# A graph kernel whose count steps start at every 4th node in place of every 8th

## What is computed

```
h  = relu(layernorm(x))
x  = x + relu([h, sum of h[src] by dst, sum of edge_attr by dst] @ W.T + b)
h  = relu(layernorm(x))
h1 = relu(mean of h[src] by dst  @ W1_l + b1 + h  @ W1_r)
x  = x + relu(mean of h1[src] by dst @ W2_l + b2 + h1 @ W2_r)
```

## Time and profile before

| | before |
|---|---|
| median of three runs | 1425.23 us |
| the profiled execution | 1426.45 us |
| its span in the trace | 1424.6 us |
| first step of the build loop starts | 113.0 us |
| last step of the build loop starts | 647.4 us |

### The profile page before, as it was taken

The page is one execution under the profiler, slowest core; times in us unless marked ns, Lnnn a source line. Parts: engine busy times, 40 slices in busy tenths (PEclk is TensorE's granted clock), DMA queues, the critical chain, the costliest instruction groups (busy, mean ns, idle before and its releaser), DMA issues.

```text
span 1424.6 us, 34949 instructions
## 1 busy us (share of the span) xinstructions
PE 1352.9 (95%) x12145; PEld 1227.3 (86%) x12146; DVE 807.9 (57%) x1830; ACT 492.1 (35%) x1398; POOL 645.4 (45%) x762
## 2 busy tenths in 40 slices
PE   3768999999999999999999999999999999999996
PEld 3657999999999999898888888888888888888885
DVE  8678999988988888883445445522222223222122
ACT  2731123455788888882333232311111110000000
POOL 5400001111112122126777776367777654777775
PEclk9688999999999999999999999999999999999998
DMA  6109778888899998895654564656656555666663
GB/s 185 28 4 255 204 221 242 236 250 244 265 273 271 273 280 263 263 278 184 231 184 162 192 222 125 210 180 200 204 188 214 184 184 189 210 216 214 220 219 87
DMA packets 284437, 293.91 MB, mean 206 GB/s; under 512 B 19317, under 2 KB 249920, under 8 KB 284384
## 3 DMA queue, kind: packets, MB, share of 16 engines
q1 hardware_dynamic: 233861, 212.90, 47.6%
q0 software_dynamic: 25728, 68.65, 16.3%
q10 hardware_dynamic: 24795, 11.74, 2.9%
HBM read 245.11 MB, written 48.11 MB: 206 GB/s over the span
## 4 chain that ended last, share of the span: by engine, by line
PE 88%; DVE 4%; ACT 3%; DMA 2%; issue 2%; POOL 2%; ACTq 0%; POOLq 0%; SPq 0%; DVEq 0%
PE edge_banks L1148 42%; PE edge_banks L1084 21%; PE banks L1058 10%; PE edge_banks L1125 4%; PE edge_banks L1080 4%; PE banks L1166 3%; POOL shared L882 2%; PE banks L946 1%; ACT own L1296 1%; DMA shared<-in_edge_attr 1%; PE edge_banks L1155 1%; PE banks L1160 1%; DVE edge_t L1508 1%; ACT shared L1353 1%; DMA shared<-g_rows,list_src 0%
## 5 line engine op out<-in xcount | busy, mean ns | idle before, releaser
L882 POOL DMA_INDIRECT shared<-g_rows,list_src x546 | 532.3, 975 | 232.9 <-issue 166.4
L1148 PE MATMUL edge_banks<-g_even,shared 128*128 128x257 f16 (+1 forms) x3822 | 443.4, 272 | 1.2 <-DVE shared L1776 1.2
L1148 PEld LDWEIGHTS edge_banks<-g_even,shared 128*128 128x128 fp8e3 x3822 | 371.6, 97 | 58.8 <-DVEq L1686 1.3
L1084 PE MATMUL edge_banks<-shared 128*128 128x128 f32 x2744 | 345.3, 276 | 5.2 <-issue 4.3
L1084 PEld LDWEIGHTS edge_banks<-shared 128*128 128x128 f32 x2744 | 325.8, 193 | 8.5 <-issue 8.1
L860 POOL DMA_DIRECT2D counts<-shared x156 | 76.5, 491 | 479.6 <-ACT shared L1353 464.7
L1737 DVE SCALAR_TENSOR_TENSOR shared<-edge_banks,shared,own 128x128 f32<-128x128 f32 x98 | 34.4, 351 | 362.2 <-PE edge_banks L1148 339.5
L1148 PE MATMUL edge_banks<-shared 128*128 128x256 f16 x1911 | 225.8, 272 | 0.2 <-DVE own L1719 0.2
L1653 DVE TENSOR_TENSOR shared<-iota,shared 128x3528 f16<-128x3528 f16 x98 | 195.4, 1994 | 38.9 <-PE banks L1058 38.5
L1353 ACT ACTIVATE shared<-banks 128x392 uint16<-128x392 f32 x312 | 152.1, 487 | 176.0 <-PE banks L1058 165.5
L1148 PEld LDWEIGHTS edge_banks<-shared 128*128 128x128 fp8e3 x1911 | 185.3, 97 | 30.7 <-DVE own L1719 0.5
(11 more groups left out here) (282 smaller groups left out, 978.1 us busy)
## 6 DMA issues: line engine op xcount, KB each, us to landing
shared<-in_edge_attr SPq DMA_DIRECT2D x195, 512.0 KB, 4.7
shared<-counts SPq DMA_DIRECT2D x117, 784.0 KB
counts<-shared POOLq DMA_DIRECT2D x156, 196.0 KB, 4.1
shared<-g_rows,list_src POOLq DMA_INDIRECT x546, 2.6
shared<-hot_rows SPq DMA_DIRECT2D x20, 304.0 KB
g_rows<-g_even SPq DMA_DIRECT2D x1, 3136.0 KB, 15.8
g_rows<-shared ACTq DMA_DIRECT2D x49, 64.0 KB
g_rows<-g_even ACTq DMA_DIRECT2D x49, 64.0 KB
```

Source lines behind the costliest of these rows:

```text
L882: pool.indirect_dma_start(ring_g[use % RING][:, t, 0:2 * D], None, g_rows[r], bass.IndirectOffsetOnAxis(ap=list_src[:, at:at + 1], axis=0) ...
L1084: mm = pe.matmul(edge_wide[bank][:, :, at], ring[:, bank * GROUP_TILES + j, :], hot_dst[u][:, k, (j - 1) * SPREAD:j * SPREAD].unsqueeze(1) ...
L1148: mm = pe.matmul(acc[s][:, 0:wide], stream8[slot][:, order[h], :], G[r % 2][:, order[h], 0:wide], start=h == 0, stop=h == BLOCKS - 1, skip ...
```

## The change

The window becomes 4 nodes wide. Counts go to the same memory in the same layout, and the other constants follow:

| | before | after |
|---|---|---|
| nodes of a window (`WIN`) | 8 | 4 |
| cells of a step, so columns of its matmul | 196 | 98 |
| stretches in a bank (`DUO`) | 2 | 4 |
| steps an iteration (`STEPS_IT`) | 18 | 20 |
| steps in the program | 1764 | 1960 |
| waits for a cleared bank in a half | 2 (before steps 1 and 6) | 1 (before step 1, for all ten) |
| window starts held by a partition (`PER`) | 7 | 10 |
| columns compared for each tile row (`MARKS`) | 912 | 1388 |
| indirect DMAs for the starts | 8 | 12 |
| blocks of 128 in the step tables (`SBLK`) | 14 | 16 |

The starts of the ten listed blocks get a column of their own (`STARTS` = `PER` + 2) in place of being picked out of all starts by seven matmuls. The edge sums, the bank count, the 312 copies and clears, and the rounds stay.

```
-WIN = 8
-DUO = 2
+WIN = 4
+DUO = 4
-SLOT = 256
-STEPS_IT = 18
+SLOT = 128
+STEPS_IT = 20
-PARTS = ((0, 5), (5, 9))
+PARTS = ((0, 5), (5, 10))
-PER = 7
+PER = 10
-SRC_BITS = 13
+SRC_BITS = 14
...
-            for j in range(PER + 1):
+            for j in range(STARTS):
                 pool.indirect_dma_start(rows8[:, j, :], None, keys_table, bass.IndirectOffsetOnAxis(ap=tw_i[:, j:j + 1], axis=0)).then_inc(S["rows8_in"], 16)
...
-                        for j in range(PER):
-                            pe.matmul(to[:, 72 + c:73 + c], pick_j[:, j, lists], first_e[:, j:j + 1], start=j == 0, stop=False, skip_group_check=True)
+                        pe.matmul(to[:, 72 + c:73 + c], pick[:, lists], first_e[0:LISTED, PER + 1:STARTS], start=True, stop=False, skip_group_check=True)
...
                         def steps(half, regs):
-                            for (lo, hi), until in zip(PARTS, regs[HALF:HALF + 2]):
+                            for lo, hi in PARTS:
                                 at = slots(regs[lo:hi])
-                                pe.wait_ge(S["zeroed"], until)
+                                if lo == 0:
+                                    pe.wait_ge(S["zeroed"], regs[HALF])
                                 for s in range(lo, hi):
...
                     def clear(j):
                         act.wait_ge(S["evacuated"], b * DPB + (j + 1))
-                        act.activation(duo[j % BANKS], zeros16[:, 0:1].unsqueeze(1).broadcast_to([P, DUO, CELLS]), ACT.Copy).then_inc(S["zeroed"], 2)
+                        act.activation(duo[j % BANKS], zeros16[:, 0:1].unsqueeze(1).broadcast_to([P, DUO, CELLS]), ACT.Copy).then_inc(S["zeroed"], DUO)
```

More of the change, by code:

```diff
@@ L224, in message_passing @@
         keys = place(4992, TCOLS).bitcast(I32).rearrange("p (b e) -> p b e", e=P)
[L225 to L228, removed]
+        IN_SHARED = 8
+        cmp16 = [(place(6656 + b * (MARKS // 2), MARKS // 2) if b < IN_SHARED else own_t[:, (b - IN_SHARED) * (MARKS // 2):(b - IN_SHARED + 1) * (MARKS // 2)]
+                  ).bitcast(F16) for b in range(TBLK)]
+        marks_i = own_t[:, 4800:4800 + MARKS].bitcast(I32)
+        marks16 = place(12828, MARKS // 2).bitcast(F16)
+        assert 6656 + IN_SHARED * (MARKS // 2) <= 12828 and 12828 + MARKS // 2 <= 14492 and (TBLK - IN_SHARED) * (MARKS // 2) <= 4800 and 4800 + MARKS <= NPAD
         iota2k = edge_t[:, 5300:5300 + SPAD // 2].bitcast(F16)
@@ L299, in message_passing @@
         next16 = small[:, 416:432].bitcast(F16)[:, 0:SBLK]
-        over = small[0:HOLDERS, 448:455]
+        over = small[0:HOLDERS, 512:512 + PER]
         col_over = small[:, 464:464 + TBLK]
@@ L304, in message_passing @@
         list_at = small[:, 500:500 + LBLK].bitcast(I32)
-        in_dense = small[0:HOLDERS, 504:512][:, 0:PER]
+        in_dense = small[0:HOLDERS, 524:524 + PER]
         banks = ctx.enter_context(nc.psum_tensor("banks", [P, BANKS, 512], F32))
@@ L816, in _ @@
             pool.memset(ones[:, :], 1.0)
-            pool.memset(place(22068, 4), 0.0)
+            pool.memset(place(22116, 4), 0.0)
             pool.memset(pairs16, 1.0)
@@ L974, in _ @@
                 if t == 1:
-                    for j in range(PER):
-                        at, odd = (PER // 2 + j // 2, 1) if j % 2 == 0 else (j // 2, 0)
-                        mm = pe.matmul(flat[1][96:97, at:at + PER * (HOLDERS // 2 - 1) + 1:PER], c_end[:, j:j + 1],
-                                       identz[0:HOLDERS, 1 + odd:HOLDERS + odd:2], start=True, stop=True, skip_group_check=True)
+                    for j in range(1, PER, 2):
+                        odd = (DUO - 1 - j) // 2 % 2
+                        at, count, stride = (PER * odd + j) // DUO, len(range(odd, HOLDERS, 2)), 2 * PER // DUO
+                        mm = pe.matmul(flat[1][96:97, at:at + stride * (count - 1) + 1:stride], c_end[:, j:j + 1],
+                                       identz[0:HOLDERS, 1 + odd:1 + HOLDERS:2], start=True, stop=True, skip_group_check=True)
                     mm.then_inc(S["rows_up"], 1)
```

132 lines of the change are left out of this document (66 added, 66 removed).

## The result

| | before | after |
|---|---|---|
| median | 1426.31 us (4 runs) | 1450.05 us (4 runs, 1447.13 to 1455.58) |
| the profiled execution | 1426.45 us | 1455.58 us |

The ratio is 1.0169, 95% interval 1.0146 to 1.0192. The sign was right; the time lies 19 us above the forecast and 7 us above the range. The two differ by 3 us in the early stretch, so a difference of that size between two single profiled executions shows little.

A forecast was written before the change was run, and what follows sets the result against it. It took PE's array as the early bound, its sequencer nearly as high, and ACT within 5% of its floor late. Build about +1 and setup about +5 gave +6 us on 1426.45, 1432.4, forecast as 1431 us, range 1417 to 1443.

The forecast's parts named there:

- Setup: Work before the first step: longer tables and sums, less a shorter L1004 and earlier first cells; about +5 us, bounds 2 and 9.
- (a): Setup: L1475, 4.77 us for 13 x 912 columns, grows with 1388 columns; +1.6 us.
- (b): Setup: POOL's number tables, 722 elements longer, delay the chain by about 1.0 us (0 to 2).
- (c) to (e): Setup: larger operations on window starts +1.1 us, twenty small matmuls for 14 +0.6, ten larger L1560 for seven +2.5.
- Early: Build loop to the end of block 14: faster iterations, pace mean 5.11 us, spent on two more iterations; 0 us.
- The floors: Each engine's shortest iteration time; early, PE's sequencer at 9.8 to 10.4 us for two iterations replaces the array's 9.68.
- Rival 1: Build loop early: PE's sequencer is no floor, pace follows the array at 4.9 us; 1418 us, chance 0.15.
- rival 2: Whole kernel: the terms cancel, pace 5.0 us early, 9.4 us a block late; 1422 us, chance 0.20.
- Late: Last 24 blocks of the build loop: ACT becomes the bound, 9.5 us a block with a little waiting; -8 us.
- Unused steps: End of the build loop: 2.9 unused iterations at 5.2 us, 15 us in place of 6.5; +8.6 us.
- The rounds: After the build loop, from 650 us: taken as they are; 0 us.
- Rivals 3 and 4: Build loop: strided load paces a step at 0.086 us, 1447 us, chance 0.08; single wait starves ACT, 1443 us, 0.12.

The follow-up runs named there:

- e2: The changed kernel with one register instruction ahead of PE's and ACT's waits on a register's value: 1450.24 us.
- e4: As e2, but ACT clears only two of a bank's four stretches (counts are other numbers): 1436.22 us.
- e10: As e2, but POOL's stores of counts write 1 of 32 rows except for the last block, whose counts the rounds read: 1432.88 us.
- e3: As e2, but a step's weight load reads 128 elements in a row in place of a distance of 20 elements: 1441.55 us.
- e9: As e2, but each PE load brings 7 words in place of 12, with ten register instructions a half left out: 1548.2 us.
- e12: The kernel before, with added register instructions ahead of waits, and PE waiting once a half ahead of its nine steps: 1431.62 us.
- e8: The kernel before, with added register instructions ahead of waits, each step streaming only 98 of its 196 columns: ratio to before 0.9949.
- e13: As e9, but PE's loads bring 8 words from the row's fifth on: ratio 0.9999 to the kernel before on that chip.
- e17: The kernel before, with added register instructions ahead of waits, ACT issuing a block's four stores of counts in place of POOL: 1561.17 us, ratio 1.0936.

## Why the prediction was wrong in size

- **Setup, +5 forecast, +9.1.** This step failed. I wrote that the twelve indirect DMAs end in time. They took 18.3 us, not twelve times the 1.23 us of before, since each takes 1.21 us with a 0.3 us gap, and POOL's subtraction behind them slid over DVE's L1533: +3.6 us. So PE's sums were ready 10.0 us later than before, where (a) to (e) gave 6.8. (a) was right (6.5 us in place of 4.8), (b) was nothing in place of 1.0, (c) to (e) gave 4.2 as forecast. The clock was no term of mine at all. The dense product at 98.95 us took twice the time of its like before, the one at the lower clock level (1.2 GHz, granted clock 0.50), the other at the higher (2.4 GHz, granted clock 1.00). Start, us and what, from the chain of waits of before and of after:

```profile
92.49 1.99 PE banks L946 x8
```

```profile
98.95 3.78 PE banks L949 x8
```

  That is +1.8 us. It is not the change's alone. This product took 3.78 us in after, e2, e4 and e10, but 1.99 and 2.00 in e3 and e9, whose first step is at 119.7 and 120.1 us and not at 122.1; and among the runs of the kernel before's form it took 3.78 us in e12, with the first step at 114.8 us, and 1.99 or 2.00 in the others on the faster chips. The chain of e3 and of e12:

```profile
98.82 1.99 PE banks L949 x8
```

```profile
92.09 3.78 PE banks L946 x8
```

  Why the clock is low there in one run and not in another was not tried. Neither cost, L1533's or the clock's, comes from an instruction that the change altered.
- **Early, 0 forecast, +2.8 in e2.** The floors were right: the sequencer took the array's place. Pace 5.14 against 5.11 forecast, 5.20 in the changed kernel's own profile, whose loads average 1.01 us against 0.98. Another 1.4 us is a slip of my sum: 536.5 less 24 x 9.85 less 1.2 x 5.4 is 293.6 us and not 295, and before took 293.9. Rival 1, no sequencer floor, fell with e3, e8, e9 and e13, and rival 2 with it: it needed 5.0 us early and 9.4 late.
- **Late, -8 forecast, -2.4.** This step failed as well. The mechanism was right (ACT becomes the bound, e4) and the size of the term wrong: 9.7 us a block for 9.5, where before was 9.8 and not 9.85. The prediction named its sign of being wrong, ACT waiting for PE, and the copies do wait 10.2 us (11.7 before). ACT's 9.4 us a block is reached only in e10, with loads of 0.86 us. With loads of up to 2 us PE arrives late at some banks, ACT waits for it, and the time is not made up: 9.7. I took the higher of two floors, with 0.1 us for waiting. ACT's was right; PE's I took as 8.3 us, and e4, which lowers ACT's floor, still takes 9.15. The coarse wait may add to that (e12).
- **Unused steps, +8.6 forecast, +11.5.** Before took 5.3 us and not 6.5, which is 1.2 us of the 2.9. The 2.9 iterations cost 14.0 us in e3 and 14.2 in e10, about my 15, but 16.8 in after and 16.9 in e2. There is one long load there, which now runs while the last block is being stored, and behind it the clock. Before, the loop had ended by then. The load, and ten microseconds behind its start with the columns of the earlier trace rows, of after:

```profile
L1097 PEldq TENSOR_LOAD <-shared x1: 3390/3390/3390, 658.9 to 658.9; - x1
```

```profile
660.00:665.00 5.00, 2.82 (x21) 2.48 (x21) 2.54 (x5) 0.00 (x0) 0.00 (x0) 0.81 0.76 220
665.00:670.00 5.00, 5.00 (x49) 5.00 (x48) 0.54 (x2) 0.00 (x0) 0.00 (x0) 0.85 0.09 27
```

  PE stands still for 2.2 us, and then the mean granted clock is under 1. In e2 PE stood still for 2.0 us, and the granted clock from 659.9 to 663.3 us was 0.50. In e10, with a load of 2.2 us, PE stood still for 1.0 us and the granted clock stayed 1.00; it did so too in e3 and e4, where PE stood still for 1.3 and 1.4 us. By these figures, of the 2.7 us between e2 and e10 the standing still is about 1.0 and 3.4 us at half the clock up to 1.7 (an estimate).
- **The rounds, 0 forecast.** In the six runs of the changed form on the faster chips the time from the last step to the end is 1.3 to 4.3 us longer than in the kernel before. In the two where it is about 4 us longer, after and e4, the mean granted clock is 0.57 from 980 to 984 us and 0.66 from 963 to 968; the other four have no such spell. I did not try why, nor where the rest comes from.
- **Rivals 3 and 4** named times near the result, 1447 and 1443, for reasons that are not the case: a step takes 0.062 us, not 0.086, and the single wait costs some 3 us (e12), not 12.

Summed, e2 is 17.9 us over my terms: setup 4.0, early 2.8, late 5.6, unused 3.0, the end 2.3, the first iterations 0.2. None of them came out lower than forecast.

## What to carry to other kernels

When two engines that feed each other have floors near each other, price the pace as the higher floor plus a few per cent, not as the higher one (here 5.28 us over 5.16 before, and 9.7 over 9.4 late after); a gain on one of them is then mostly eaten by the other. A table that grows in setup moves what follows it: look at each instruction that slides, on the other engines too, for what it now runs beside. And a padded loop pays for each unused turn at the full pace.

## What the runs showed of the hardware

- A TENSOR_LOAD of PE's sequencer took 0.85 us for 12 words, 1.62 for 24, 0.59 for 8, and 1.70 for 7; DVE's of 4 words took 0.34. That fits 0.34 us for the first four words and 0.26 for each further four, and 0.24 for each single word at 7, the one count tried that is no multiple of four. The Trainium skill ("DMA: Bandwidth & Descriptors", "Latency and other measured facts") gives a floor of some 600 ns and says that the compiler unrolls by four; the 0.34 us and 0.59 us here are below it.
- The loads of 12 words grow, to 3.4 us after the change and to 3.8 in e17, while counts are being stored to memory: mean late 1.11 us, and 0.86 without most of the stores (e10). Before the first store, in the first three iterations, the longest is 2.7 us in before and 3.0 in after.
- An indirect DMA of POOL took 0.93 us for 112 rows, 0.94 for 128, and 1.21 for 125.
- A weight load with a distance of 20 elements between columns took 158 ns beside a step of 98 columns, and 98 ns in a row, where a step then follows every 0.046 us in place of 0.062 (e3); with a distance of 18 it took 157 beside a step of 98 columns (e8) and 141 beside one of 196.
- Eight matmuls of the dense product took 1.99 to 2.01 us at granted clock 1.00 and 3.78 at 0.50.
